# First mixture of an audio tower: the tokens' shares reach all partitions by a list in DRAM read back broadcast, in place of eight matrix products and two copies a group

## Chip, core and metric

The kernel runs on one core of a Trainium2 chip. The metric is the device time of one execution in microseconds; the time before is the median of three runs. The engines are PE (TensorE, matrix products), DVE (VectorE), ACT (ScalarE), POOL (GpSimd) and SP (SyncE, which here only starts DMAs). On-chip memory (SBUF) has 128 partitions; PE writes its products to PSUM.

## What is computed

The program is a whole tower: a token mixer, a retention layer, a first mixture of experts, a distance attention and a second mixture of experts, each with a residual. Only the first mixture is touched:

```python
def _L0_ffn_ref(x, Wg, W1, b1, W2, b2):
    K = 2
    logits = jnp.einsum('btd,de->bte', x, Wg)
    probs = jax.nn.softmax(logits, axis=-1)
    top_p, _top_i = jax.lax.top_k(probs, K)
    top_p = top_p / jnp.sum(top_p, axis=-1, keepdims=True)
    b2_sum = jnp.sum(b2, axis=0)
    out = jnp.zeros_like(x)
    for i in range(K):
        w_in = x * top_p[..., i:i + 1]
        h = jax.nn.gelu(jnp.einsum('btd,edf->ebtf', w_in, W1) + b1[:, None, None, :], approximate=False)
        out = out + jnp.einsum('ebtf,efd->btd', h, W2) + b2_sum
    return out
```

There are 8 experts with 512 hidden units each, a width of 128, and 6144 token slots. Every token runs through all experts twice, once scaled by its larger and once by its smaller normalised share. Those two numbers per token are the shares of this document.

## The kernel before

The phase `phase_first_mixture` handles the tokens in 12 groups of 512 (`N`), held as columns: 128 partitions are the features, 512 columns the tokens. A group has 32 steps (`NQ`: 8 experts by 4 blocks of 128 hidden units). A step runs through all engines in a chain:

- PE, `up(g, q)`: three products (L1204 to L1206) that give 128 hidden units for 512 tokens in the PSUM tile `p_h`, one of four.
- DVE, `scale` (L1342): multiplies them by both shares into `scaled`, 128 x 1024. It reads `shares`, a tile of 128 x 2 x 512 in which every partition holds all 512 tokens' two shares. There are two such tiles, for even and odd groups.
- ACT (L1266): bias and gelu into `hid`.
- POOL (L1295): adds the two halves into `both`.
- PE, `down(g, q)` (L1211): the product with the second weights, accumulated in `p_o`. It is issued six steps behind `up` (`LAG`), and PE's own order within a step is up, then down.

`up(g, q)` waits until DVE has done the scaling four steps earlier, since there are four `p_h` tiles.

The next group is prepared inside the 32 steps of the running one, at fixed step numbers. DVE copies the residual stream (L619, after step 1), does statistics (after step 5) and normalises (step 9), PE transposes (steps 4 and 12), DVE splits the result for the products (step 14), PE makes the router's logits (`route`, step 17, L1187) in the PSUM tile `p_b`, DVE takes the two best (step 17), POOL the power (step 17), and DVE `share_out` (step 21, L1333 to L1337) the two shares. These lie in the small tile `share`, 128 partitions x 2 x 4: token n*128+p of the group has its shares on partition p. `scale` needs them in the other layout, the same row on all partitions.

Before, `spread` (PE, step 25, L1197) does that: four products of a broadcast column of `share` with the identity fill `p_b` with the first share of all tokens, ACT copies `p_b` to `shares` (`copy_shares`, L1260, issued behind its gelu of step 24), then four more products and another copy give the second share. The second four products wait for the first copy, as both use `p_b`. ACT's wait `s_bcc` also holds back the next `route`.

SP loads the phase's weights at its start and then does nothing until the phase ends. The groups 1 to 10 run as five passes of a loop over pairs; group 0 and group 11 are written out. In group 0 DVE also splits the last half of the first weights, after steps 4 and 12. Group 11 prepares no further group, so that there are 12 spreads, one ahead of group 0 and eleven inside groups 0 to 10.

Of the kernel before, what the change touches and what calls it, by code (L numbers as in the profile page):

```python
# [8 lines left out]
F32 = mybir.dt.float32  # L9
# [15 lines left out]
NG = NB // GB  # L25
N = GB * SP
# [643 lines left out]
def phase_retention(nc, sems, used, w, hT, ident, slots):  # L670

    signals = []
    with ExitStack() as ctx:
# [82 lines left out]

        CONST = 16 * 7

        @block.tensor
        def _(pe):  # L760
            ln.to_rows(pe, 0)
            ln.to_columns(pe, 0)
            pe.wait_ge(s_const, CONST)
            pe.wait_ge(s_neg, 1)
# [249 lines left out]
        def _(dve):  # L1014
# [11 lines left out]
            negative_mean(0)  # L1026
            dve.wait_ge(s_const, CONST)
            dve.wait_ge(s_zero, 4)
# [78 lines left out]
def phase_first_mixture(nc, sems, used, w, hT, ident):  # L1107

    N, ROWS, NG = WIDE, 128, NB * SP // WIDE
    signals = []  # L1110
    with ExitStack() as ctx:
# [6 lines left out]
        def sem(name):  # L1118
            signals.append(sems.enter_context(nc.semaphore("c_" + name)))
            return signals[-1]  # L1120

        NQ = E0 * NF
        SLOTS, LAG = 4, 6
# [18 lines left out]
        share = sb("share", [ROWS, 2, GB])  # L1142
        shares = [sb(f"shares{i}", [128, 2, N]) for i in range(2)]
# [6 lines left out]
        p_t, p_b = pb("p_t"), pb("p_b")  # L1150
# [3 lines left out]
        s_xhi, s_xlo, s_route, s_top, s_gap, s_odds, s_total, s_first, s_share = (  # L1154
            sem("x_hi"), sem("x_lo"), sem("gate_logits"), sem("top"), sem("gap"), sem("odds"), sem("total"),
            sem("first_share"), sem("share"))
        s_bc, s_bcc = sem("share_rows"), sem("shares")
        s_up, s_sc, s_ge, s_bo, s_down = sem("up"), sem("scaled"), sem("gelu"), sem("both"), sem("down")
        s_h, s_set, s_b2, s_b2b = sem("h"), sem("set"), sem("b2_sum"), sem("b2_both")

        h_flat = hT[:, :, :].rearrange("p n s -> p (n s)")
        block = ctx.enter_context(nc.Block())

        def groups(eng, body):
# [8 lines left out]
        def _(sp):  # L1173
# [2 lines left out]
            sp.dma_start(w1[:, :, :], w["fW1"]).then_inc(s_w1in, 16)  # L1176
            sp.dma_start(w2[:, :, :], w["fW2"]).then_inc(s_w2in, 16)

        CONST = 16 * 3

        @block.tensor
        def _(pe):
            def route(g):
                pe.wait_ge(ln.s_xT, g + 1)
                pe.wait_ge(s_bcc, 2 * g)
                for n in range(GB):
                    last = nc.tensor.matmul(p_b[0:ROWS, n * E0:(n + 1) * E0], ln.xT[:, n * ROWS:(n + 1) * ROWS], wg[:, :],  # L1187
                                            start=True, stop=True, skip_group_check=True)
                last.then_inc(s_route, 1)

            def spread(g):
                pe.wait_ge(s_share, g + 1)
                for i in range(2):
                    if i == 1:
                        pe.wait_ge(s_bcc, 2 * g + 1)
                    for n in range(GB):
                        last = nc.tensor.matmul(p_b[:, n * ROWS:(n + 1) * ROWS],  # L1197
                                                share[:, i, n:n + 1].to_broadcast([ROWS, 128]), ident[0:ROWS, 0:ROWS],
                                                start=True, stop=True, skip_group_check=True)
                    last.then_inc(s_bc, 1)  # L1200

            def up(g, q, s):
                pe.wait_ge(s_sc, NQ * g + q + 1)
                nc.tensor.matmul(p_h[q % SLOTS][:, 0:N], w1_hi[:, q, :], x_hi[s][:, :], start=True, stop=False)  # L1204
                nc.tensor.matmul(p_h[q % SLOTS][:, 0:N], w1_hi[:, q, :], x_lo[s][:, :], start=False, stop=False)  # L1205
                nc.tensor.matmul(p_h[q % SLOTS][:, 0:N], w1_lo[:, q, :], x_hi[s][:, :], start=False, stop=True)\  # L1206
                    .then_inc(s_up, 1)

            def down(g, q, s):
                pe.wait_ge(s_bo, NQ * g + q + 1 + SLOTS)  # L1210
                nc.tensor.matmul(p_o[s][:, 0:N], w2[:, q, :], both[q % SLOTS][:, :], start=(q == 0),  # L1211
                                 stop=(q == NQ - 1)).then_inc(s_down, 1)

            def body(g, s, before, after):
                pe.wait_ge(s_xlo, g + 1)
                for q in range(NQ):
                    if not before:
                        if q % (NQ // PIECES) == 0:
                            pe.wait_ge(s_split, q // (NQ // PIECES) + 1)
                        if q == LAG:  # L1220
                            pe.wait_ge(s_w2in, 16)
                    up(g, q, s)
                    if q < LAG:
                        if before:
                            down(g - 1, q + NQ - LAG, 1 - s)
                    else:
                        if q == LAG and before:
                            pe.wait_ge(s_h, g)
                        down(g, q - LAG, s)
                    if after:  # L1230
                        if q == 4:
                            ln.to_rows(pe, g + 1)
                        if q == 12:
                            ln.to_columns(pe, g + 1)
                        if q == 17:
                            route(g + 1)
                        if q == 25:
                            spread(g + 1)

            pe.sem_inc(s_down, SLOTS)  # L1240
            ln.to_rows(pe, 0)
            ln.to_columns(pe, 0)
            pe.wait_ge(s_const, CONST)
            route(0)
            spread(0)
            groups(pe, body)
            for q in range(NQ - LAG, NQ):
                down(NG - 1, q, 1)

        @block.scalar  # L1250
        def _(act):
            act.sem_inc(s_ge, SLOTS)
            act.wait_ge(s_const, CONST)

            def copy_shares(g, s):
                for i in range(2):
                    act.wait_ge(s_bc, 2 * g + i + 1)
                    if not (isinstance(g, int) and g < 2):
                        act.wait_ge(s_sc, NQ * (g - 1) + SLOTS)
                    nc.scalar.copy(shares[s][:, i, :], p_b[:, 0:N]).then_inc(s_bcc, 1)  # L1260

            def body(g, s, before, after):
                for q in range(NQ):
                    act.wait_ge(s_sc, NQ * g + q + 1 + SLOTS)
                    act.wait_ge(s_bo, NQ * g + q + 1)
                    nc.scalar.activation(hid[q % SLOTS][:, :, :], scaled[q % SLOTS][:, :, :], ACT.Gelu,  # L1266
                                         bias=b1[:, q:q + 1]).then_inc(s_ge, 1)
                    if after:
                        if q == 12:
                            ln.copy_out(act, g + 1)  # L1270
                        if q == 24:
                            copy_shares(g + 1, 1 - s)

            ln.copy_out(act, 0)
            copy_shares(0, 0)
            groups(act, body)

        @block.gpsimd
# [29 lines left out]
        def _(dve):  # L1308
# [20 lines left out]

            def share_out(g):  # L1330
                dve.wait_ge(s_odds, g + 1)
                dve.wait_ge(s_bc, 2 * g)
                v.tensor_scalar(total[:, :], odds[:, :], 1.0, None, ALU.add).then_inc(s_total, 1)  # L1333
                dve.wait_ge(s_total, g + 1)
                v.reciprocal(share[:, 0, :], total[:, :]).then_inc(s_first, 1)
                dve.wait_ge(s_first, g + 1)
                v.tensor_tensor(share[:, 1, :], share[:, 0, :], odds[:, :], ALU.mult).then_inc(s_share, 1)  # L1337
# [34 lines left out]

            def body(g, s, before, after):
                if before:
                    dve.wait_ge(s_bcc, 2 * g + 2)
                for q in range(NQ):
                    scale(g, q, s)
                    if not before and q in (4, 12):
                        split_w(2 if q == 4 else 3)
                    if q == LAG + 1 and before:  # L1380
                        store_h(g - 1, 1 - s)
                    if after:
                        if q == 1:
                            ln.copy_in(dve, g + 1, h_flat[:, bass.ds((g + 1) * N, N)])
                        if q == 5:
                            ln.statistics(dve, g + 1)
                        if q == 9:
                            ln.normalise(dve, g + 1)
                        if q == 14:
                            split_x(g + 1, 1 - s)  # L1390
                        if q == 17:
                            best(g + 1)
                        if q == 21:
                            share_out(g + 1)
# [1350 lines left out]
```

## Time and profile before

| | us |
|---|---|
| median of 3 runs | 2219.95 (2216.2 to 2221.93) |
| span of the profiled execution | 2216.8 |
| of it the first mixture's groups | about 740 to 1396 |
| a group in the middle of it | 54.33 |

The profile is of one execution, whose span is the time from its first to its last instruction. It gives for each engine the busy time, for each group of instructions the mean duration and the idle time ahead with what ended it, and a timeline of single instructions. The end of a matrix product is modelled, so the starts of products are what distances are read from. A letter x with a number is a count.

### The profile page before, as it was taken

The page shows a single profiled execution, that of the slowest core. Times are in us where ns is not written, and L with a number is a line of the kernel's source. Part 1 is how long each engine was busy: PE and PEld are TensorE (multiplying, and loading weights), DVE is VectorE, ACT ScalarE, POOL GpSimd, SP SyncE. Part 2 cuts the span into 40 slices and gives each one's busy share as a digit, 9 for nine tenths or more (in the row PEclk, how much of TensorE's full clock was granted, in tenths as well). Part 3 has the DMA queues.
Part 4 walks back from the last instruction along what each step waited for, and adds up shares of the span by engine and source line. Part 5 has one row for each costly group of instructions (what it writes and reads, how often), then busy time and mean ns, then how long its engine had stood idle before and what let it go on. Part 6 is the DMA issues. An engine that isn't in the chain of part 4 may idle for free. (4 is left out here: it accounts for less than half of the span.)

```text
span 2216.8 us, 48165 instructions
## 1 busy us (share of the span) xinstructions
PE 1939.5 (87%) x16762; PEld 1352.9 (61%) x16762; DVE 1543.1 (70%) x3606; ACT 1319.0 (60%) x2379; POOL 883.1 (40%) x733
## 2 busy tenths in 40 slices
PE   6899999979997799999999999799999995676881
PEld 5778887845554466666666666466666663454660
DVE  5534445357775888888888887577777775666774
ACT  2445446445553477766777667577777774564771
POOL 0000000014444577777777777100000001776772
PEclk9999999989998899999999999999999995779995
DMA  8861010049910100000000000000000002214885
GB/s 291 327 220 30 20 30 11 1 178 419 420 68 1 77 1 1 0 0 0 0 0 0 0 0 0 23 1 0 0 0 0 0 1 67 80 46 136 233 232 183
DMA packets 78111, 171.54 MB, mean 77 GB/s; under 512 B 13678, under 2 KB 56991, under 8 KB 68615
## 3 DMA queue, kind: packets, MB, share of 16 engines
q1 hardware_dynamic: 65446, 154.26, 19.9%
q0 software_dynamic: 6624, 12.70, 1.7%
q10 hardware_dynamic: 5888, 2.62, 0.4%
q8 instruction: 87, 1.43, 0.3%
q14 instruction: 66, 0.53, 0.1%
HBM read 75.70 MB, written 94.81 MB: 77 GB/s over the span
## 5 line engine op out<-in xcount | busy, mean ns | idle before, releaser
L1295 POOL TENSOR_TENSOR c_both<-c_hid 128x512 f32<-128x512 f32 x384 | 494.5, 1295 | 144.8 <-ACT c_hid L1266 108.3
L1266 ACT ACTIVATE c_hid<-c_scaled,c_b 128x1024 f32<-128x1024 f32 x384 | 437.2, 1150 | 176.6 <-DVE c_scaled L1342 162.3
L1342 DVE TENSOR_TENSOR c_scaled<-c_p_h,c_shares 128x1024 f32<-128x1024 f32 x384 | 454.7, 1217 | 80.2 <-PE c_p_h L1206 79.0
L1211 PE MATMUL c_p_o<-c_both,c_w 128*128 128x512 f32 x768 | 390.8, 592 | 0.0
L1204 PE MATMUL c_p_h<-c_x_hi,c_w_hi 128*128 128x512 f32 x384 | 289.8, 755 | 4.0 <-DVE c_scaled L1342 4.0
L647 POOL TENSOR_TENSOR d_ln_rstd<-d_ln_var,d_ln_power 128x2 f32<-128x2 f32 x48 | 34.1, 710 | 417.1 <-DVE d_ln_var L643 417.1
L1211 PEld LDWEIGHTS c_p_o<-c_both,c_w 128*128 128x128 f32 x768 | 144.4, 188 | 35.9 <-issue 2.2
L1051 DVE TENSOR_TENSOR b_sm<-b_p_s,b_decay 96x384 f32<-96x384 f32 x256 | 124.6, 546 | 46.5 <-PE b_p_s L780 46.5
L1205 PE MATMUL c_p_h<-c_x_lo,c_w_hi 128*128 128x512 f32 x384 | 151.9, 395 | 0.0
L1206 PE MATMUL c_p_h<-c_x_hi,c_w_lo 128*128 128x512 f32 x384 | 151.4, 394 | 0.0
L249 POOL COPY a_work<-a_vec 128x64 f32<-128x64 f32 x4 | 1.2, 303 | 376.6 <-PE a_p_A L340 222.9
L2389 POOL DMA_INDIRECT e_again<-e_by,e_bid x111 | 109.0, 982 | 46.5 <-ACT e_by L2345 22.8
L1204 PEld LDWEIGHTS c_p_h<-c_x_hi,c_w_hi 128*128 128x128 f32 x384 | 73.0, 190 | 87.6 <-issue 73.5
L1205 PEld LDWEIGHTS c_p_h<-c_x_lo,c_w_hi 128*128 128x128 f32 x384 | 73.3, 191 | 79.0 <-issue 78.7
L2381 POOL DMA_INDIRECT slots<-e_rows_x,e_pos x96 | 96.1, 1001 | 34.8 <-issue 24.2
L1805 DVE TENSOR_SCALAR d_kk<-d_p_p,d_mu 128x256 f32<-128x256 f32 x96 | 46.0, 479 | 87.7 <-PE d_p_p L1521 87.7
L1009 POOL TENSOR_TENSOR b_yrs<-b_yve,b_power 96x32 f32<-96x32 f32 x16 | 86.8, 5423 | 50.3 <-DVE b_yve L1060 50.3
L324 PE MATMUL a_p_A<-a_R,a_V 128*128 128x128 f32 x496 | 96.2, 276 | 0.0
L326 PE MATMUL a_p_A<-a_R,a_V 128*128 128x128 f32 x496 | 96.0, 275 | 0.0
L528 DVE COPY a_work<-a_p_A 128x512 f32<-128x512 f32 (+1 forms) x32 | 21.6, 676 | 99.6 <-PE a_p_A L326 99.6
L1206 PEld LDWEIGHTS c_p_h<-c_x_hi,c_w_lo 128*128 128x128 f32 x384 | 72.3, 188 | 18.1
L521 DVE COPY a_V<-a_p_V 128x500 f32<-128x500 f32 x80 | 52.1, 673 | 39.7 <-PE a_p_V L278 39.7
(324 smaller groups left out, 4558.1 us busy)
## 6 DMA issues: line engine op xcount, KB each, us to landing
slots<-b_blank SPq DMA_DIRECT2D x55, 1040.0 KB, 23.6
e_wb<-e_weights SPq DMA_DIRECT2D x111, 164.0 KB
band_scratch<-a_work SPq DMA_DIRECT2D x16, 1024.0 KB, 5.4
a_work<-band_scratch SPq DMA_DIRECT2D x16, 1023.5 KB, 7.8
a_raw<-in_Wc SPq DMA_DIRECT2D x16, 512.0 KB, 3.9
e_xb<-slots SPq DMA_DIRECT2D x111, 65.0 KB
e_yb<-e_again SPq DMA_DIRECT2D x12, 512.0 KB, 5.8
a_work<-in_x_tok SPq DMA_DIRECT2D x16, 256.0 KB, 3.1
```

The lines of the kernel that those rows point to most:

```text
L324: nc.tensor.matmul(bank[:, cols], V[:, j, :], R[:, f, 0:2 * NB], start=True, stop=False, skip_group_check=True)
L326: last = nc.tensor.matmul(bank[:, cols], V[:, j + 1, :], R[:, f, NB:3 * NB], start=False, stop=True, skip_group_check=True)
L1051: v.tensor_tensor(sm[n % 2][:, j, :], p_s[j][0:SP, 0:4 * SP], decay[:, j, :, :].rearrange("t a s -> t (a s)"), ALU.mult).then_inc(s_sm, 1)
L1204: nc.tensor.matmul(p_h[q % SLOTS][:, 0:N], w1_hi[:, q, :], x_hi[s][:, :], start=True, stop=False)
L1205: nc.tensor.matmul(p_h[q % SLOTS][:, 0:N], w1_hi[:, q, :], x_lo[s][:, :], start=False, stop=False)
L1206: nc.tensor.matmul(p_h[q % SLOTS][:, 0:N], w1_lo[:, q, :], x_hi[s][:, :], start=False, stop=True)\
L1211: nc.tensor.matmul(p_o[s][:, 0:N], w2[:, q, :], both[q % SLOTS][:, :], start=(q == 0), stop=(q == NQ - 1)).then_inc(s_down, 1)
L1266: nc.scalar.activation(hid[q % SLOTS][:, :, :], scaled[q % SLOTS][:, :, :], ACT.Gelu, bias=b1[:, q:q + 1]).then_inc(s_ge, 1)
L1295: nc.gpsimd.tensor_tensor(both[q % SLOTS][:, :], hid[q % SLOTS][:, 0, :], hid[q % SLOTS][:, 1, :], ALU.add).then_inc(s_bo, 1)
L1342: v.tensor_tensor(scaled[q % SLOTS][:, :, :], p_h[q % SLOTS][:, 0:N].unsqueeze(1).to_broadcast([128, 2, N]), shares[s][:, :, :], ALU.mult) ...
L2381: nc.gpsimd.indirect_dma_start(out=slots, out_offset=bass.IndirectOffsetOnAxis(ap=pos[g % RX][:, i * GB + n:i * GB + n + 1], axis=0), in_= ...
L2389: nc.gpsimd.indirect_dma_start(out=again, out_offset=bass.IndirectOffsetOnAxis(ap=bid[k % RY][:, 0:1], axis=0), in_=by[k % RY][:, :], in_o ...
```

## The change

For groups 1 to 11 the eight products and the two copies are gone. SP does the work instead. When `share` is written it starts two DMAs that write the 512 first shares and the 512 second shares as a row of 1024 numbers into a DRAM tensor (`c_share_lists`, two rows, for even and odd groups). When both have landed, it starts a third DMA that reads the row back to all 128 partitions, straight into `shares`. Group 0 keeps the products and copies (`spread_first`, `first_shares`). DVE waits ahead of a group's first `scale` for the third DMA (`s_spread`) instead of the copies; `route` waits for DVE's reading of `p_b` (`s_top`) instead of the copies, and `share_out` for the previous group's two list DMAs (`s_kept`).

```diff
+        lists = nc.dram_tensor("c_share_lists", (2, 2 * N), F32, kind="Internal").ap()
...
+            for g in range(1, NG):
+                sp.wait_ge(s_share, g + 1)
+                if g >= 2:
+                    sp.wait_ge(s_spread, 16 * (g - 1))
+                for i in range(2):
+                    sp.dma_start(lists[g % 2, i * N:(i + 1) * N].rearrange("(n p) -> p n", p=ROWS), share[:, i, :],
+                                 allow_slow_non_contiguous=True)\
+                        .then_inc(s_kept, 16)
+                sp.wait_ge(s_kept, 16 * 2 * g)
+                if g >= 2:
+                    sp.wait_ge(s_sc, NQ * (g - 1) + SLOTS)
+                sp.dma_start(shares[g % 2][:, :, :].rearrange("p i n -> p (i n)"), lists[g % 2].partition_broadcast(128))\
+                    .then_inc(s_spread, 16)
...
             def route(g):
                 pe.wait_ge(ln.s_xT, g + 1)
-                pe.wait_ge(s_bcc, 2 * g)
+                if isinstance(g, int) and g == 1:
+                    pe.wait_ge(s_bcc, 2)
+                elif not isinstance(g, int):
+                    pe.wait_ge(s_top, g)
...
-                        if q == 25:
-                            spread(g + 1)
...
-                        if q == 24:
-                            copy_shares(g + 1, 1 - s)
...
             def share_out(g):
                 dve.wait_ge(s_odds, g + 1)
-                dve.wait_ge(s_bc, 2 * g)
+                if isinstance(g, int) and g == 1:
+                    dve.wait_ge(s_bc, 2)
+                elif not isinstance(g, int):
+                    dve.wait_ge(s_kept, 16 * 2 * (g - 1))
...
                 if before:
-                    dve.wait_ge(s_bcc, 2 * g + 2)
+                    dve.wait_ge(s_spread, 16 * g)
```

What the change moves in PE's row of instructions, at steps 25 and 26 of a group in the loop. The down product L1211 (L1230 after) ends step 25, and the three up products behind begin step 26. Before:

```order
L1211 MATMUL c_p_o<-c_both,c_w 128x512
L1197 MATMUL c_p_b<-identity,c_share 128x128 x4
L1195 REGISTER_ALU
L1197 MATMUL c_p_b<-identity,c_share 128x128 x4
L1203 REGISTER_ALU
L1204 MATMUL c_p_h<-c_x_hi,c_w_hi 128x512
```

After:

```order
L1230 MATMUL c_p_o<-c_both,c_w 128x512
L1222 REGISTER_ALU
L1223 MATMUL c_p_h<-c_x_hi,c_w_hi 128x512
L1224 MATMUL c_p_h<-c_x_lo,c_w_hi 128x512
L1225 MATMUL c_p_h<-c_x_hi,c_w_lo 128x512
```

The eight products between the down product of step 25 and the up products of step 26 are gone, with the wait between their halves.

In SP's row, between the loading of the phase's weights and the end of the phase, first before, where nothing stood (the last two rows are the way to the next phase):

```order
L1176 DMA c_w<-in_fW 128x4096
L1177 DMA c_w<-in_fW 128x4096
L1111 UNCONDITIONAL_BRANCH
L1499 UNCONDITIONAL_BRANCH
L1504 DMA d_wq<-in_aWq 128x512
```

After:

```order
L1178 DMA c_w<-in_fW 128x4096
L1179 DMA c_w<-in_fW 128x4096
L1186 DMA c_share_lists<-c_share 128x4x1 x2
L1192 DMA c_shares<-c_share_lists 128x1024
L1186 DMA c_share_lists<-c_share 128x4x1 x2
L1192 DMA c_shares<-c_share_lists 128x1024
```

Eleven such pairs of rows stand there, one for each of the groups 1 to 11: two list DMAs whose pieces are single numbers, and one broadcast.

## Rows read from the trace of the kernel before

**Rows 1.** The page: span, then busy time, share and instructions of each engine.

```profile
span 2216.8 us, 48165 instructions
...
PE 1939.5 (87%) x16762; PEld 1352.9 (61%) x16762; DVE 1543.1 (70%) x3606; ACT 1319.0 (60%) x2379; POOL 883.1 (40%) x733
```

**Rows 2.** Stages: us; busy us (count) by engine; clock, DMA.

```profile
core 0: us, PE busy (x) PEld busy (x) DVE busy (x) ACT busy (x) POOL busy (x), PEclk, DMA share, GB/s
740.00:787.00 47.00, 40.20 (x148) 24.55 (x147) 44.73 (x54) 30.17 (x28) 35.49 (x26) 1.00 0.00 1
1010.00:1064.33 54.33, 53.66 (x193) 33.72 (x192) 47.66 (x58) 37.84 (x36) 42.86 (x35) 1.00 0.00 0
```

**Rows 3.** Timeline, PE, a middle group.

```profile
start us, us, engine line op out<-in xcount [idle before <-releaser]
...
1029.30 0.80 PE L1204 MATMUL c_p_h<-c_x_hi,c_w_hi 128*128 128x512 f32 x1
...
1053.51 1.02 PE L1211 MATMUL c_p_o<-c_both,c_w 128*128 128x512 f32 x2
...
1055.06 1.02 PE L1211 MATMUL c_p_o<-c_both,c_w 128*128 128x512 f32 x2
...
1057.64 1.16 PE L1197 MATMUL c_p_b<-identity,c_share 128*128 128x128 f32 x8 [0.67 <-ACT c_shares L1260]
...
1059.34 1.02 PE L1211 MATMUL c_p_o<-c_both,c_w 128*128 128x512 f32 x2
```

**Rows 4.** Timeline, PE, group 0.

```profile
779.90 1.02 PE L1211 MATMUL c_p_o<-c_both,c_w 128*128 128x512 f32 x2
...
781.45 1.02 PE L1211 MATMUL c_p_o<-c_both,c_w 128*128 128x512 f32 x2
...
787.80 1.02 PE L1211 MATMUL c_p_o<-c_both,c_w 128*128 128x512 f32 x2
```

**Rows 5.** Timeline, DVE, the same middle group and the next one's start.

```profile
1016.13 1.23 DVE L1342 TENSOR_TENSOR c_scaled<-c_p_h,c_shares 128x1024 f32<-128x1024 f32 x1 [0.34 <-PE c_p_h L1206]
...
1022.80 1.22 DVE L1342 TENSOR_TENSOR c_scaled<-c_p_h,c_shares 128x1024 f32<-128x1024 f32 x1 [0.74 <-PE c_p_h L1206]
...
1026.54 2.34 DVE L1342 TENSOR_TENSOR c_scaled<-c_p_h,c_shares 128x1024 f32<-128x1024 f32 x2
...
1050.72 0.98 DVE L1337 TENSOR_TENSOR c_share<-c_share,c_odds 128x4 f32<-128x4 f32 x1
...
1059.54 1.23 DVE L1342 TENSOR_TENSOR c_scaled<-c_p_h,c_shares 128x1024 f32<-128x1024 f32 x1 [3.06 <-PE c_p_h L1206]
...
1068.89 1.23 DVE L1342 TENSOR_TENSOR c_scaled<-c_p_h,c_shares 128x1024 f32<-128x1024 f32 x1 [0.33 <-PE c_p_h L1206]
...
1071.60 1.39 DVE L619 COPY c_ln_hg<-hT 128x512 f32 x1
```

**Rows 6.** Timeline, DVE, group 0 and the next one's start.

```profile
780.02 0.98 DVE L1337 TENSOR_TENSOR c_share<-c_share,c_odds 128x4 f32<-128x4 f32 x1
780.92 4.61 DVE L1342 TENSOR_TENSOR c_scaled<-c_p_h,c_shares 128x1024 f32<-128x1024 f32 x4
788.00 1.23 DVE L1342 TENSOR_TENSOR c_scaled<-c_p_h,c_shares 128x1024 f32<-128x1024 f32 x1 [2.48 <-PE c_p_h L1206]
...
797.30 1.23 DVE L1342 TENSOR_TENSOR c_scaled<-c_p_h,c_shares 128x1024 f32<-128x1024 f32 x1 [0.33 <-PE c_p_h L1206]
```

**Rows 7.** DMA, page: packets, MB, share; issues: KB, us to landing.

```profile
q0 software_dynamic: 6624, 12.70, 1.7%
q10 hardware_dynamic: 5888, 2.62, 0.4%
...
a_raw<-in_Wc SPq DMA_DIRECT2D x16, 512.0 KB, 3.9
...
e_yb<-e_again SPq DMA_DIRECT2D x12, 512.0 KB, 5.8
```

**Rows 8.** DMA issues of the whole span, columns as above.

```profile
out<-e_acc SPq DMA_DIRECT2D x16, 30.0 KB, 3.3
```

More of the change, by code:

```diff
@@ L1157, in phase_first_mixture @@
         s_bc, s_bcc = sem("share_rows"), sem("shares")
+        s_kept, s_spread = sem("shares_in_dram"), sem("shares_spread")
         s_up, s_sc, s_ge, s_bo, s_down = sem("up"), sem("scaled"), sem("gelu"), sem("both"), sem("down")
@@ L1189, in route, with spread_first @@
                 last.then_inc(s_route, 1)
-            def spread(g):
-                pe.wait_ge(s_share, g + 1)
+            def spread_first():
+                pe.wait_ge(s_share, 1)
                 for i in range(2):
                     if i == 1:
-                        pe.wait_ge(s_bcc, 2 * g + 1)
+                        pe.wait_ge(s_bcc, 1)
                     for n in range(GB):
@@ L1244, in _ @@
             route(0)
-            spread(0)
+            spread_first()
             groups(pe, body)
@@ L1253, in _, with first_shares @@
             act.wait_ge(s_const, CONST)
-            def copy_shares(g, s):
+            def first_shares():
                 for i in range(2):
[L1257 to L1260, printed above, removed]
+                    act.wait_ge(s_bc, i + 1)
+                    nc.scalar.copy(shares[0][:, i, :], p_b[:, 0:N]).then_inc(s_bcc, 1)
             def body(g, s, before, after):
@@ L1270, in body @@
                             ln.copy_out(act, g + 1)
-                        if q == 24:
-                            copy_shares(g + 1, 1 - s)
             ln.copy_out(act, 0)
-            copy_shares(0, 0)
+            first_shares()
             groups(act, body)
```

## The prediction, made before the changed kernel ran

> **What bounds the kernel now.** I read the page's first part for the execution's own time, 2216.8 us [rows 1], and then only the stretch that the change touches. The table by stages gives the bound there: in a middle group, 54.33 us long, PE is busy for 53.66 us at a granted clock of 1.00, DVE for 47.66, POOL for 42.86, ACT for 37.84, and the DMA engines carry nothing [rows 2]. So PE sets the pace, DVE comes next. In group 0, which also splits weights on DVE, it is the other way round for much of the time: DVE 44.73 of 47.00 us, PE 40.20 [rows 2].
>
> PE's timeline shows how a middle group's 54.33 us are made up. From one down product to the next it is 1.55 us (1053.51 to 1055.06) in a step without extras. From the down product of step 25 (1055.06) to that of step 26 (1059.34) it is 4.28 us [rows 3]. Between them stand the eight spread products and 0.67 us of waiting for the first copy [rows 3]. DVE's timeline shows the echo: it idles 3.06 us ahead of the `scale` at 1059.54, for PE [rows 5]. A thing that stands on the path of the engine that sets the pace, and has no other work under it, is worth its whole length.
>
> **What the change removes.** In each of the groups 1 to 10 the distance at the spread falls from 4.28 to 1.55 us: 2.73 us, times 10 = 27.3 us. I read all ten distances; they run from 4.27 to 4.28, and one of them is in the rows [rows 3]. Group 0 is dearer: from 781.45 to 787.80, 6.35 us against 1.55 in its neighbour, so 4.80 us [rows 4], since ACT makes the first copy only behind the gelu of step 24, which follows DVE's late `scale` of step 24. That is 27.3 + 4.8 = 32.1 us of PE's time.
>
> Does all of it come through? `up` waits for the `scale` four steps earlier. In a middle group DVE's idle times of a third of a microsecond ahead of single `scale`s, 0.34 at 1016.13, show that it had caught up [rows 5]; without the pause it keeps 54.33 - 2.73 = 51.60 us for 47.66 us of work, so it is not the bound. In group 0 DVE is behind: four `scale`s without a gap from 780.92 to 785.53 (steps 22 to 25), then 2.48 us of idling [rows 6]. It will go straight on. Steps 26 to 31 at 4.61 / 4 = 1.15 us each end at 785.53 + 6.9 = 792.4. PE, for its part, would have the first product of group 1 ready 4.80 us earlier than now, when DVE takes it at 797.30, so at 792.50 [rows 6]. The two meet, and group 0 gives its 4.8 us; its lower bound is DVE's 2.48 us, if DVE stays the bound. The two copies on ACT and the issue work are off the path, at nothing: ACT has 16 us free in a group [rows 2].
>
> **What it adds: a round trip over DRAM.** The path is: DVE writes `share`; SP starts two list DMAs; both land; SP starts the broadcast; it lands; DVE may begin the next group. Queued behind this wait on DVE is the first `scale`, and behind it the copy of the stream, the statistics, all of the next group. PE is held only when it wants a fifth `p_h` tile.
>
> How much time is there? In a middle group `share` is written at 1050.72 + 0.98 = 1051.70. The next group's first `scale` is the second ahead of the copy at 1071.60, so at 1068.89 [rows 5]; without the pause it moves to 1066.16. That leaves **14.5 us**. From group 0 to 1 it is 781.00 to 792.50, **11.5 us** [rows 6].
>
> A late start costs nothing at once. Where DVE is furthest behind today, `up` of step 10 starts at 1029.30 [rows 3] and needs the `scale` of step 6, the first of the two from 1026.54, done at 1027.71 [rows 5]: 1.6 us to spare. Before that DVE idles 0.34 and 0.74 us [rows 5], together 1.1. So some 2.7 us of lateness are absorbed, and the limits are 14.5 + 2.7 = 17.2 us and 11.5 + 2.7 = 14.2 us. At a later stage of the group DVE makes it up from its 51.60 - 47.66 = 3.9 us.
>
> How long is the trip? No row shows a DMA of single numbers, so I bound it. The list DMAs move 1024 packets of 4 bytes, 64 for each of 16 DMA engines. A small store to DRAM, 30 KB from SP, lands in 3.3 us [rows 8]. To that come 64 packets at a price between that of the small packets of q10, 0.4% of 16 x 2216.8 us over 5888 packets = 24 ns, and that of q0, 1.7% over 6624 = 91 ns [rows 7]: 1.5 to 5.8 us. The broadcast moves 512 KB; loads of that size land in 3.9 us (`a_raw`) and 5.8 us (`e_yb`) [rows 7]. The ends are 3.3 + 1.5 + 3.9 = 8.7 us and 3.3 + 5.8 + 5.8 = 14.9 us. I take about 10 us, near the lower end: the DMA engines are idle in this stage [rows 2], and q10 is the queue of plain stores as these are. That fits into 11.5 and 14.5. Even the upper end passes a middle group and costs only 0.7 us once, in group 0. One thing no row bounds: 1024 numbers written next to each other in one 4 KB stretch of DRAM, and 128 reads of the same 4 KB.
>
> On these packets a rule speaks against the change. The rows show whole rows of numbers as packets, never single ones [rows 7]. The Trainium skill, page "DMA: Bandwidth & Descriptors", section "Rules for kernel authors", says that a strided last dimension becomes one descriptor for each element and should be rearranged, and it calls a plain DMA with a rearranged access pattern 19 times slower than the hardware transpose. Its section "Anatomy of one DMA" gives a fit of about 2.0 us and bytes over 436 GB/s a DMA; by that the trip would be some 2.0 + 2.0 + 1.2 = 5.2 us (an estimate), inside the time there is. By the first rule it is the second rival below.
>
> **The sum.** 27.3 + 4.8 - 0 = 32.1 us off the path. The span goes from 2216.8 to 2184.7. The median of the runs lies 3.15 us above this span, so 2219.95 - 32.1 = **2187.9 us**.
>
> **The rivals.** *DVE becomes the bound.* For: at 47.66 of 51.60 us it is 92% busy, its work is bunched in steps 1 to 21, where PE's margin is down to 1.6 us, and in group 0 it was behind. Against: the middle groups' bunched stretch comes before the pause, not behind it, and PE's step there is the plain 1.55 us today. If each group loses half of what is removed, 16 us come: 2204 us. Chance 0.08.
>
> *The list is slow enough to cost the gain and more.* It would be one mechanism: single numbers written beside each other into DRAM don't overlap, neither on an engine nor between engines. The broadcast waits for both lists on SP, DVE waits for the broadcast, and PE stops at the fifth product of the next group. It starts to cost at 17.2 us and decides the sign at 17.2 + 2.7 = 19.9 us. At a tenth of a whole small store for each of the 64 packets, 0.33 us, the lists take 3.3 + 21.1 = 24.4 us and the trip 24.4 + 5.8 = 30.2: 13.0 us too late ten times and 16.0 once, 146 - 32 = 114 us slower, **2334 us**. The Trainium skill's 19 times (page "DMA: Bandwidth & Descriptors", section "Rules for kernel authors"), laid on a whole small store, would lie further out on the same side, some 60 us a list (an estimate). For: nothing in the rows shows such packets, and neighbouring numbers come from different engines' writes. Against: 24 and 91 ns a packet are what other packets take here [rows 7]. Chance 0.11, spread from 2225 up.
>
> *The trip takes 17.2 to 19.9 us.* Then the lateness eats part of each group's 2.7 us; at 18.5 us it is 1.3 x 10 + 4.3 = 17 us back, 2205 us. Chance 0.07.
>
> *The change doesn't reach the path*, since PE waits somewhere else for the same time: the only waits that the edit leaves on PE there are those for `scale` and `both`, which rows 3 show unheld. That is the first rival's case, and has no chance of its own.
>
> **How the numbers follow.** Full gain 0.74, DVE 0.08, part of the gain 0.07, slower 0.11. A measurement of this kernel tells about 0.3%, 6.7 us, from no change. Full gain and DVE are faster by more; of the partial case 0.05 is, 0.02 is within it; of the slow case 0.01 is within it. So faster 0.87, within 0.3% 0.03, slower 0.10. The full gain's own spread is 29.7 (group 0 at 2.48) to 32.1 us, and the runs before spread by 3.8 us down and 2.0 us up from their median: 2184 to 2192. For 8 in 10 the range takes in the DVE case and the partial one's middle: **2183 to 2206 us**.
>
> **What would show it.** PE's timeline: the distance at step 25 to 26 is 1.55 us, a middle group 51.6 us long, PE's idle time nil. The DMA rows: list DMAs landing in some 5 us, the broadcast in 4 to 6, so that DVE's first `scale` of a group is released by PE's product and not by a DMA. In group 1 the first `scale` comes near 792.5. It is wrong if `scale` waits for a DMA for more than 2.7 us in middle groups, if PE waits for `scale` at steps 10 to 12, or if a granted clock under 1.00 appears in the stage.

## The result, and the profile after

The changed kernel takes 2185.11 us (median of 4 runs, 2184.37 to 2186.13), against 2218.07 us (median of 4, 2215.96 to 2221.93) for the kernel before: ratio 0.9842, 95% interval 0.9831 to 0.9854. That is 33 us or 1.6% less. The profiled execution's span fell from 2216.8 to 2182.6 us. The forecast was 2187.9 us.

First the page and the table by stages of the changed kernel, answering to [rows 1] and [rows 2]:

```profile
span 2182.6 us, 47795 instructions
...
PE 1919.2 (88%) x16586; PEld 1335.6 (61%) x16586; DVE 1540.7 (71%) x3606; ACT 1307.1 (60%) x2357; POOL 883.2 (40%) x733
```

```profile
core 0: us, PE busy (x) PEld busy (x) DVE busy (x) ACT busy (x) POOL busy (x), PEclk, DMA share, GB/s
...
1010.00:1064.00 54.00, 54.00 (x187) 33.41 (x185) 49.94 (x67) 37.90 (x34) 45.05 (x36) 1.00 0.05 10
```

In the middle of the mixture PE is now busy all the time at a granted clock of 1.00, and DVE for 49.94 of 54 us, up from 47.66 of 54.33: the same work in shorter groups, so that the stretch holds a little more than one. The DMA engines, idle in this stage before, carry 10 GB/s.

Three neighbouring down products of PE in a middle group, those of steps 24, 25 and 26; the spread stood between the last two in [rows 3]:

```profile
1039.72 1.02 PE L1230 MATMUL c_p_o<-c_both,c_w 128*128 128x512 f32 x2
...
1041.27 1.02 PE L1230 MATMUL c_p_o<-c_both,c_w 128*128 128x512 f32 x2
...
1042.82 1.02 PE L1230 MATMUL c_p_o<-c_both,c_w 128*128 128x512 f32 x2
```

Each is 1.55 us behind the last; between the last two it was 4.28 us before.

DVE's timeline of the same group, answering to [rows 5]. The copies L619 mark one place in each group:

```profile
1003.51 1.39 DVE L619 COPY c_ln_hg<-hT 128x512 f32 x1
...
1036.92 0.98 DVE L1353 TENSOR_TENSOR c_share<-c_share,c_odds 128x4 f32<-128x4 f32 x1
...
1052.32 1.22 DVE L1358 TENSOR_TENSOR c_scaled<-c_p_h,c_shares 128x1024 f32<-128x1024 f32 x1 [0.32 <-PE c_p_h L1225]
1053.87 1.23 DVE L1358 TENSOR_TENSOR c_scaled<-c_p_h,c_shares 128x1024 f32<-128x1024 f32 x1 [0.33 <-PE c_p_h L1225]
1055.01 1.39 DVE L619 COPY c_ln_hg<-hT 128x512 f32 x1
```

From copy to copy it is 1055.01 - 1003.51 = 51.50 us, before 54.33. The shares are written at 1036.92 + 0.98 = 1037.90, and the next group's first `scale` (1052.32) is released by PE, not by a DMA.

How the trip went, from SP's queue (start, time in the queue) and from the table of DMA issues (KB each, median us from issue to landing; the lists' number is for one of the two):

```profile
783.20 0.93 SPq L1186 DMA_DIRECT2D c_share_lists<-c_share  x2
791.83 0.33 SPq L1192 DMA_DIRECT2D c_shares<-c_share_lists  x1
...
1037.94 0.91 SPq L1186 DMA_DIRECT2D c_share_lists<-c_share  x2
1047.10 0.33 SPq L1192 DMA_DIRECT2D c_shares<-c_share_lists  x1
```

```profile
c_shares<-c_share_lists SPq DMA_DIRECT2D x11, 512.0 KB, 4.0
c_share_lists<-c_share SPq DMA_DIRECT2D x22, 2.0 KB, 8.7
```

In the middle group the lists were issued at 1037.94, had both landed by 1047.10, and the broadcast took about 4.0 us more: 13.2 us from the writing of the shares, 1.2 us before they were wanted at 1052.32. I had said about 10. This trip is one of the shorter ones: over the eleven groups the time from issuing the lists to issuing the broadcast runs from 8.6 to 10.7 us, so that trips reach 14.7 us, and behind two later groups DVE waited 0.58 and 0.52 us for the DMA.

Behind group 0 it was too late. DVE's timeline, answering to [rows 6], then the copy after that, then what DVE and PE waited for in all (total us, times, longest):

```profile
782.20 0.97 DVE L1353 TENSOR_TENSOR c_share<-c_share,c_odds 128x4 f32<-128x4 f32 x1
783.10 11.39 DVE L1358 TENSOR_TENSOR c_scaled<-c_p_h,c_shares 128x1024 f32<-128x1024 f32 x10
797.55 2.36 DVE L1358 TENSOR_TENSOR c_scaled<-c_p_h,c_shares 128x1024 f32<-128x1024 f32 x2 [3.07 <-DMA c_shares<-c_share_lists]
799.82 0.42 DVE L619 COPY c_ln_hg<-hT 128x512 f32 x1
```

```profile
849.01 1.40 DVE L619 COPY c_ln_hg<-hT 128x512 f32 x1
```

```profile
DVE c_scaled L1358 <- DMA c_shares<-c_share_lists: 4.2, 3, 3.1
...
PE c_p_h L1223 <- DVE c_scaled L1358: 3.3, 2, 1.9
```

DVE stood 3.07 us for the DMA, though it ran from 783.10 through ten `scale`s without a gap. The copy after that tells that nothing was lost: from 799.82 to 849.01 only 49.19 us passed, less than a settled group's 51.50. In total DVE waited 4.2 us for DMAs, in three places, and the 3.3 us for which PE waited for DVE (4.0 before) are, as before, in group 0 (at 752.79 and 756.47), behind DVE's splitting of the weights.

### The profile page after: what moved, and what is told of

It reads as the page before. It is cut to its first block and busy times, and to the rows that moved or that the text cites. A ratio compares the mean times of both kernels' runs of the same rounds, so it can differ in the third digit from the quotient of the medians.

```text
span 2182.6 us, 47795 instructions
## 1 busy us (share of the span) xinstructions
PE 1919.2 (88%) x16586; PEld 1335.6 (61%) x16586; DVE 1540.7 (71%) x3606; ACT 1307.1 (60%) x2357; POOL 883.2 (40%) x733
## 5 line engine op out<-in xcount | busy, mean ns | idle before, releaser
L1358 DVE TENSOR_TENSOR c_scaled<-c_p_h,c_shares 128x1024 f32<-128x1024 f32 x384 | 453.8, 1215 | 49.3 <-PE c_p_h L1225 44.1
L1230 PE MATMUL c_p_o<-c_both,c_w 128*128 128x512 f32 x768 | 391.7, 593 | 0.0
L1230 PEld LDWEIGHTS c_p_o<-c_both,c_w 128*128 128x128 f32 x768 | 144.8, 189 | 35.6 <-issue 2.2
```

The lines of the kernel that those rows point to most:

```text
L1358: v.tensor_tensor(scaled[q % SLOTS][:, :, :], p_h[q % SLOTS][:, 0:N].unsqueeze(1).to_broadcast([128, 2, N]), shares[s][:, :, :], ALU.mult) ...
```

## The experiments

All are compared with the kernel before on the chip that they ran on. Three of them (the list far apart, half the list, and the last one) ran on a chip where the kernel before takes 2285.71 us, about 3% longer; from these only ratios, single distances and the landing times of DMAs are used.

**The changed kernel again**, as the yardstick:

> The changed kernel once more, as the yardstick for the others on the same chip: 2185 us, 0.984 to 0.985 of the kernel before, by either theory.

2185.97 us, ratio 0.9842 (0.9828 to 0.9855).

**No trip at all.** The three DMAs are gone, and every group reads the first group's tile, so the shares of groups 1 to 11 are left out:

```diff
-            for g in range(1, NG):
-                sp.wait_ge(s_share, g + 1)
...
-                if before:
-                    dve.wait_ge(s_spread, 16 * g)
...
-                                shares[s][:, :, :], ALU.mult).then_inc(s_sc, 1)
+                                shares[0][:, :, :], ALU.mult).then_inc(s_sc, 1)
```

> The changed kernel without the three DMAs and without DVE's wait for them: all groups are scaled by group 0's shares, so this leaves out the shares of groups 1 to 11. Theory A (the trip is wholly under other work, and the waits of 3.07, 0.58 and 0.52 us that DVE spends for it are made up later): the same time as the changed kernel within 1 us, 2185. Theory B (what DVE waits for the DMAs reaches the end, or the traffic slows the engines): 4 us or more faster, 2181 or less.

2186.10 us, ratio 0.9845 (0.9832 to 0.9859). The copies in two neighbouring groups of DVE's timeline:

```profile
1002.13 1.39 DVE L619 COPY c_ln_hg<-hT 128x512 f32 x1
...
1053.63 1.39 DVE L619 COPY c_ln_hg<-hT 128x512 f32 x1
```

The same 51.50 us. Here the copies of groups 0 and 1 are 52.74 us apart and the next distance is 51.50, together 104.24; with the trip it was 55.11 + 49.19 = 104.30. So the trip, its traffic and DVE's 4.2 us of waiting cost nothing that can be told: theory A. The whole 33 us come from what was removed, and a faster trip would not add to it.

**A longer trip.** The broadcast is done twice, or three times, each after the last has landed (`{k}` is 2 or 3):

```diff
+                for turn in range({k}):
+                    if turn > 0:
+                        sp.wait_ge(s_spread, 16 * ({k} * (g - 1) + turn))
+                    sp.dma_start(shares[g % 2][:, :, :].rearrange("p i n -> p (i n)"), lists[g % 2].partition_broadcast(128))\
+                        .then_inc(s_spread, 16)
...
+                    dve.wait_ge(s_spread, 16 * {k} * g)
```

> The broadcast is done twice, one behind the other's landing, before DVE may begin: the trip grows by about 4.4 us, from 13.2 to 17.6 in a middle group and from 14.4 to 18.8 behind group 0. With the 2.7 us of lateness that I said are absorbed (limits 17.2 and 14.2): 0.4 us late in ten groups and 4.6 once, some 8 us more than the changed kernel, 2193. If every microsecond beyond 14.4 (11.4 behind group 0) costs, with no cushion: 3.2 x 10 + 7 = 39 more, 2224. If the four product tiles cushion more than I think (4 us and up): 2186 to 2188.

> Three broadcasts in a row: the trip is 22.0 us in a middle group and 23.2 behind group 0. With the cushion of 2.7 us: 4.8 x 10 + 9.0 = 57 more, 2242, slower than the kernel before. Without a cushion 2264 to 2270. With one of over 4 us 2225 or less.

Two reads: 2200.77 us, ratio 0.9915 (0.9896 to 0.9933), about 15 us more than the changed kernel. Three: 2246.82 us, ratio 1.0120 (1.0102 to 1.0138), about 61 us more and slower than the kernel before. Both lie far below the figures without a cushion (2224 and 2264), and a little above mine (2193 and 2242). DVE's timelines show the law that I had only approximated: a group's first `scale`, its writing of the shares, and the next group's first `scale`. With two reads:

```profile
1010.78 2.36 DVE L1361 TENSOR_TENSOR c_scaled<-c_p_h,c_shares 128x1024 f32<-128x1024 f32 x2 [5.38 <-DMA c_shares<-c_share_lists]
...
1044.60 0.98 DVE L1356 TENSOR_TENSOR c_share<-c_share,c_odds 128x4 f32<-128x4 f32 x1
...
1063.07 2.36 DVE L1361 TENSOR_TENSOR c_scaled<-c_p_h,c_shares 128x1024 f32<-128x1024 f32 x2 [5.04 <-PE c_p_h L1228]
```

With three:

```profile
1035.52 2.36 DVE L1361 TENSOR_TENSOR c_scaled<-c_p_h,c_shares 128x1024 f32<-128x1024 f32 x2 [7.71 <-DMA c_shares<-c_share_lists]
...
1069.36 0.98 DVE L1356 TENSOR_TENSOR c_share<-c_share,c_odds 128x4 f32<-128x4 f32 x1
...
1091.82 2.36 DVE L1361 TENSOR_TENSOR c_scaled<-c_p_h,c_shares 128x1024 f32<-128x1024 f32 x2 [9.04 <-DMA c_shares<-c_share_lists]
```

Two reads: 1010.78 to 1045.58 is 34.8 us of DVE's work from the first `scale` to the shares, then 17.5 us of trip, a group of 52.3 us. Three: 34.8 and 21.5 us, a group of 56.3 us. (With two reads the wait at 1063.07 is put down to PE, whose tile had long been ready; the broadcast came last.) DVE's wait for the trip and its writing of the next shares form a ring, and once it is late DVE does its 34.8 us without a gap. So a group takes the longer of PE's 51.5 us and 34.8 us plus the trip. These two groups are among the shortest of their kernels, since the trip varies from group to group: with two reads the ten distances run from 52.3 to 53.1 us (mean 52.7), with three from 55.9 to 58.1 (mean 56.8). The 34.8 us are read from the same two traces, so what these kernels show is that DVE's part stays the same while the trip grows, and that the lateness comes back in every group. Worked out from that, the trip is free up to 51.5 - 34.8 = 16.7 us and reaches the old 54.3 us at 19.5; no run had a trip of just that length. Against 16.7 the changed kernel's 13.2 us in the middle group leave 3.5 to spare, its longest trip of 14.7 leaves 2.0.

**Fewer packets for the list.** One DMA writes it in the order of the partitions, and the readers take the shares with a step of eight numbers:

```diff
-                for i in range(2):
-                    sp.dma_start(lists[g % 2, i * N:(i + 1) * N].rearrange("(n p) -> p n", p=ROWS), share[:, i, :],
...
+                sp.dma_start(lists[g % 2].rearrange("(p k) -> p k", p=ROWS), share[:, :, :].rearrange("p i n -> p (i n)"))\
...
+            return t[:, :, :].rearrange("c i n -> c (i n)").rearrange("c (p i n) -> c i n p", p=ROWS, i=2)
```

> The list is written by one DMA in the order of the partitions, 128 packets of 32 bytes in place of 1024 of 4 bytes, and DVE reads the shares with a step of eight numbers. If the packets' number makes the list slow, it lands in 3 to 4 us in place of 8.7, and DVE never waits for a DMA. Theory A: the time stays at 2185, since the trip was hidden already. Theory B: 2181 or less. If the stepped read costs DVE time, a scale takes more than 1.15 us; above 1.3 us DVE becomes the bound and the kernel gets slower than the changed one.

2432.41 us, ratio 1.0951 (1.0935 to 1.0967). The table of DMA issues:

```profile
c_shares<-c_share_lists SPq DMA_DIRECT2D x11, 512.0 KB, 3.7
...
c_share_lists<-c_share SPq DMA_DIRECT2D x11, 4.0 KB, 1.4
```

The list lands in 1.4 us, less than the 3 to 4 that I expected. But the groups of lines (count | busy us, mean ns | idle before):

```profile
L1360 DVE TENSOR_TENSOR c_scaled<-c_p_h,c_shares 128x1024 f32<-128x1024 f32 x381 | 765.4, 2093 | 3.0 <-PE c_p_h L1226 3.0
...
L1224 PE MATMUL c_p_h<-c_x_hi,c_w_hi 128*128 128x512 f32 x384 | 199.9, 521 | 115.7 <-DVE c_scaled L1360 115.1
```

A `scale` with the stepped read takes 2093 ns instead of 1215, and PE waits 115.1 us for it. The group is now DVE's: in a middle one DVE is busy for 71.98 of 72.32 us. The instruction also works in runs of 128 numbers instead of 512, which this run doesn't separate from the step. This also shows the first rival's mechanism at work, at a size that the change never had.

**Is it the number of packets, or that they lie side by side?** First the same 1024 packets, each 64 bytes from the next. The broadcast then reads other numbers, so the shares of groups 1 to 11 are left out:

```diff
-        lists = nc.dram_tensor("c_share_lists", (2, 2 * N), F32, kind="Internal").ap()
+        lists = nc.dram_tensor("c_share_lists", (2, 2 * N, 16), F32, kind="Internal").ap()
...
-                    sp.dma_start(lists[g % 2, i * N:(i + 1) * N].rearrange("(n p) -> p n", p=ROWS), share[:, i, :],
+                    sp.dma_start(lists[g % 2, i * N:(i + 1) * N, 0].rearrange("(n p) -> p n", p=ROWS), share[:, i, :],
...
-                sp.dma_start(shares[g % 2][:, :, :].rearrange("p i n -> p (i n)"), lists[g % 2].partition_broadcast(128))\
+                sp.dma_start(shares[g % 2][:, :, :].rearrange("p i n -> p (i n)"), w["fW2"][0, 0:8, :].rearrange("q h -> (q h)").partition_broadcast(128))\
```

> The same 1024 packets of 4 bytes, but each to an address of its own 64 bytes apart, in place of side by side in 4 KB; the broadcast reads 1024 other numbers (a row of the second weights), so the shares of groups 1 to 11 are left out. If the list takes 8.7 us because the engines need that long for 64 packets each: 8 to 9 us again, 2186. If writes side by side get in each other's way: 3 to 5 us.

```profile
c_share_lists<-c_share SPq DMA_DIRECT2D x22, 2.0 KB, 1.9
```

Then only the first of the two lists, side by side as in the changed kernel, with the same broadcast of other numbers and with the waits set for one list:

```diff
-                for i in range(2):
+                for i in range(1):
```

> Only the first shares' list is written, 512 packets of 4 bytes, 32 for each DMA engine, and the broadcast again reads other numbers; the shares of groups 1 to 11 are left out. If the packets set the time, above a small fixed part of about 1.4 us (what 128 packets of 32 bytes took): 1.4 + (8.7 - 1.4) / 2 = 5 us. If it is a fixed cost of such a DMA: 8 us.

```profile
c_share_lists<-c_share SPq DMA_DIRECT2D x11, 2.0 KB, 8.3
```

1.9 us when they lie apart, 8.3 us for half as many when they lie side by side (medians of 22 and of 11 DMAs; each kernel ran once, 2247.92 and 2251.62 us, 0.983 and 0.985 of the kernel before). So the number of packets hardly matters here; what costs some 7 us is that single numbers are written next to each other. The theories that counted packets fall, and so does a fixed cost of such a DMA, since the lists far apart are DMAs of the same kind. The packets of 32 bytes, also side by side, landed in 1.4 us.

The changed kernel's own trace tells when those 7 us pass. Its DMA packets in the microsecond behind the issue at 1037.94 (packets, MB, share of the engines), then two stretches from there to the issue of the broadcast, with the columns of the table by stages:

```profile
q1 hardware_dynamic: 1056, 0.00, 50.7%
```

```profile
1038.80:1039.80 1.00, 1.00 (x5) 0.65 (x4) 1.00 (x2) 0.72 (x1) 0.78 (x2) 1.00 0.51 4
1039.80:1047.10 7.30, 7.30 (x25) 4.35 (x24) 6.16 (x6) 6.14 (x6) 5.96 (x6) 1.00 0.00 0
```

All 1056 packets of the two lists (the 1024 numbers and 32 more) fall within 1038.80 to 1039.80, and then no DMA packet is recorded for 7.3 us, until the lists count as landed. So the DMA engines are through with the numbers in a microsecond, and the time passes between that and the landing. What holds such writes up there isn't settled by these runs; only one distance, 64 bytes, was tried.

**The kernel before, without its wait between the halves.** The second half of the spread goes to the normalisation's PSUM tile, free at that step. The edit changes all twelve spreads, the one ahead of group 0 too:

```diff
                 for i in range(2):
-                    if i == 1:
-                        pe.wait_ge(s_bcc, 2 * g + 1)
                     for n in range(GB):
-                        last = nc.tensor.matmul(p_b[:, n * ROWS:(n + 1) * ROWS],
+                        last = nc.tensor.matmul((p_b, p_t)[i][:, n * ROWS:(n + 1) * ROWS],
...
-                    nc.scalar.copy(shares[s][:, i, :], p_b[:, 0:N]).then_inc(s_bcc, 1)
+                    nc.scalar.copy(shares[s][:, i, :], (p_b, p_t)[i][:, 0:N]).then_inc(s_bcc, 1)
```

> The kernel before, with the second half of the spread in another PSUM tile (the normalisation's, free at that step), so that PE does not wait for the first copy. If the products and that wait are each on the path at full length, PE gives up 0.67 us in ten groups and 2.75 in group 0: 9.5 us less than before, 2208.5, ratio 0.9957. If the wait is slack that returns elsewhere: 2218, no change.

2203.96 us, ratio 0.9925 (0.9911 to 0.9938): 16 us less, more than the 9.5 I gave it. PE's timeline of a middle group:

```profile
1048.65 1.02 PE L1209 MATMUL c_p_o<-c_both,c_w 128*128 128x512 f32 x2
1049.51 1.05 PE L1195 MATMUL c_p_b<-identity,c_share 128*128 128x128 f32 x8
1050.40 1.06 PE L1195 MATMUL c_p_t<-identity,c_share 128*128 128x128 f32 x8
...
1051.98 1.02 PE L1209 MATMUL c_p_o<-c_both,c_w 128*128 128x512 f32 x2
```

From down product to down product it is now 3.33 us, against 4.28 in [rows 3]: the wait was worth 0.95 us, not the 0.67 that stands as idle time ahead of the second half. In group 0 the distance fell from 6.35 to 3.35 us. That makes 0.95 x 10 + 3.0 = 12.5 us. My expectation had left out the twelfth spread, the one ahead of group 0. These are its first product and the first up product behind it, in the kernel before and then here:

```profile
734.03 2.08 PE L1197 MATMUL c_p_b<-identity,c_share 128*128 128x128 f32 x8 [2.50 <-DVE c_share L1337]
...
738.50 0.77 PE L1204 MATMUL c_p_h<-c_x_hi,c_w_hi 128*128 128x512 f32 x1
```

```profile
736.29 2.08 PE L1195 MATMUL c_p_b<-identity,c_share 128*128 128x128 f32 x8 [2.50 <-DVE c_share L1335]
...
739.73 0.55 PE L1202 MATMUL c_p_h<-c_x_hi,c_w_hi 128*128 128x512 f32 x1
```

They are 3.44 us apart here, 4.47 before, another 1.0 us. The copies L619 give a group of 53.29 us, 1.04 less than 54.33, so 0.9 us more in ten groups. Together that is some 14.4 us. The interval of the ratio stands for 13.8 to 19.8 us, so it holds this sum, but not the 12.5 alone. So of the 2.73 us that the change takes out of a group, 1.78 are the products and 0.95 the wait, and a gain of about half the size was to be had without DRAM.

**The changed kernel with that in its one spread**, ahead of group 0:

```diff
-                    if i == 1:
-                        pe.wait_ge(s_bcc, 1)
...
-                        last = nc.tensor.matmul(p_b[:, n * ROWS:(n + 1) * ROWS],
+                        last = nc.tensor.matmul((p_b, p_t)[i][:, n * ROWS:(n + 1) * ROWS],
...
-                    nc.scalar.copy(shares[0][:, i, :], p_b[:, 0:N]).then_inc(s_bcc, 1)
+                    nc.scalar.copy(shares[0][:, i, :], (p_b, p_t)[i][:, 0:N]).then_inc(s_bcc, 1)
```

> The changed kernel, with the second half of the one spread that is left, ahead of group 0, in the normalisation's PSUM tile, so that PE does not wait for the first copy (0.68 us in the profile). By the last run of this kind, in which taking away a wait of 0.67 us gave 0.95 us between two down products, the first up product comes 1 to 1.5 us earlier and the kernel takes 2184 to 2185, at the edge of what can be told; if DVE's splitting of the weights is what is late there, nothing.

Ratio 0.9845 (0.9824 to 0.9866), on the other chip: not to be told from the changed kernel's 0.9842. PE's timeline ahead of group 0, the changed kernel and this one:

```profile
736.23 2.08 PE L1216 MATMUL c_p_b<-identity,c_share 128*128 128x128 f32 x8 [2.50 <-DVE c_share L1353]
738.98 2.08 PE L1216 MATMUL c_p_b<-identity,c_share 128*128 128x128 f32 x8 [0.68 <-ACT c_shares L1275]
740.71 0.77 PE L1223 MATMUL c_p_h<-c_x_hi,c_w_hi 128*128 128x512 f32 x1
```

```profile
735.44 2.08 PE L1214 MATMUL c_p_b<-identity,c_share 128*128 128x128 f32 x8 [2.50 <-DVE c_share L1351]
737.31 1.91 PE L1214 MATMUL c_p_t<-identity,c_share 128*128 128x128 f32 x8
738.88 0.77 PE L1221 MATMUL c_p_h<-c_x_hi,c_w_hi 128*128 128x512 f32 x1
```

From the first spread product to the first up product it is 3.44 us instead of 4.48. The microsecond is there, but too small for this measurement.

## Why the prediction was right, point by point

**The bound.** PE set the pace, and what stood in its row was worth its length. 2.73 us for each of ten groups was 2.83 by the copies, 51.50 us a group for the 51.60 that I gave. For the other 0.1 us see the last section.

**Group 0.** The 4.80 us came, but not where I put them. The copies of groups 0, 1 and 2 before:

```profile
742.50 0.42 DVE L619 COPY c_ln_hg<-hT 128x512 f32<-128x512 f32 x1
...
799.98 1.39 DVE L619 COPY c_ln_hg<-hT 128x512 f32 x1
...
854.29 1.39 DVE L619 COPY c_ln_hg<-hT 128x512 f32 x1
```

I had the first `scale` of group 1 at PE's pace, near 792.5; it came at 797.55, 2.2 us of which are a later start of the whole group, and it waited 3.07 us for the DMA. After the change the copies of groups 0 and 1 stand at 744.71 and 799.82, 55.11 us apart, 2.37 less than the 57.48 before. The next distance is 49.19 us against 54.31, 5.12 less. Together 7.49 us, for the 4.80 + 2.73 = 7.53 forecast. DVE ran on from step 22 without a gap, as expected.

**The trip.** Here a term was mis-sized, and it is the one that I had no row for. I took 3.3 us for a small store and 1.5 us for the packets, 4.8 in all; the lists took 8.7, near the upper bound of 9.1. That the bound held is luck: I had built it from a price for each packet (and from q10, while the lists went over q1), and half the packets took 8.3 us. What I had named as bounded by no row, the numbers next to each other in DRAM, is the whole of the excess: far apart the same lists land in 1.9 us, less than my 4.8. The broadcast took 4.0 us, where I had bounds of 3.9 and 5.8. The trip was 13.2 us in the middle group instead of 10, with some 0.5 us of hand-over that my sum has no term for, and fitted the 14.5; the longest of 14.7 missed it by 0.2, inside the 2.7 that I took for the cushion.

**The cushion.** I gave 17.2 us as the trip that a middle group can bear and 19.9 as the point at which the gain is gone. The ring of 34.8 us and the trip gives 16.7 and 19.5, as two kernels with longer trips bear out. My way, adding up the single slack at step 10 and the idle time ahead of it, counted what one late start may cost, and not that the lateness is handed from group to group.

**The slower rival** was right that writes side by side hold each other up, here by 7 us, and wrong on how it adds up: half the packets take nearly as long (8.3 us), and the DMA engines are through with all of them in a microsecond, so it isn't a price for each packet on an engine. Which engine writes which number no run shows. From 13.2 us, 6.3 us more in every trip would have undone the gain by the ring, and the three reads, with trips of 21 us and more, did lose it. **The DVE rival** did not come up: DVE works 47.6 of 51.5 us and the bunched stretch, steps 1 to 21, was paced as before.

**The Trainium skill.** "DMA: Bandwidth & Descriptors", section "Rules for kernel authors", warns of the strided last dimension for its count of descriptors. Here the trace doesn't bear out the count: 1024 of them land in 1.9 us when they lie apart. The section "Anatomy of one DMA" gives its fit for DMAs issued by GpSimd; carried over to these from SP, a transfer of 2 or 4 KB would cost 2.0 us and the broadcast 3.2 (estimates). 1.4 and 1.9 us are near, 8.7 is not, and the broadcast took 4.0.

## What to carry to other kernels

Where one engine sets the pace, moving a small layout change off it to the idle DMA engines gains its full length, if the whole trip fits between the writing of the data and its use; work that distance out before anything else. Where the consumer also produces the next round's data, the test is not the slack at one place but the ring: its own work from use to production, plus the trip, must be shorter than the round. Before going through DRAM, look for the cheap half: a second buffer against the wait between two halves gave 16 us here, where the whole change gave 33.

## What the runs showed that I had not expected

- 512 single numbers of 4 bytes written side by side to DRAM land in 8.3 us, 1024 in two lists in 8.7 us; 1024 at a distance of 64 bytes land in 1.9 us, and 128 packets of 32 bytes, side by side, in 1.4 us. In the 8.7 us the DMA engines are at work for about one; then the lists' landing is 7.3 us away with no packet recorded.
- DVE's multiplication of 128 x 1024 takes 2093 ns instead of 1215 when one operand is read with a step of 32 bytes, in runs of 128 numbers. The Trainium skill, "SBUF — State Buffer", section "Door 1: The DMA port swizzle", has it that SBUF is read in lines of 16 bytes and that at least two hits on a line are needed for full rate; a step of 32 bytes has one, and the trace agrees in direction.
- A wait on PE costs more than the idle time recorded ahead of the product: 0.67 us recorded, 0.95 us between the products around it.
- Before, PE's plain step is 1.55 us in the steps 18 to 25 of a group and 1.56 us in the others; after the change the steps from 26 to 4 of the next group run at 1.55 too, some eleven steps of 0.01 us, which is the 0.1 us a group that the sum lacked. The kernel before without its wait has them too, which makes its 1.04 us a group out of 0.95. What switches between the two I can't tell.
